# Choosing the next operation from one token, loading the odd strips earlier, and moving TensorE's fillers

## What is computed

```
x = x + _L0_conv_ref(_ln_c(x), ...)           # two convolutions, two L1-distance convolutions
t = _to_tokens(x)
t = t + _L0_ffn_ref(_ln_t(t), ...)            # the steps below
x = x + _L1_conv_ref(_ln_c(x), ...)           # two quantised convolutions
t = t + _L1_ffn_ref(_ln_t(t), ...)            # long filters over the tokens, mixed
```

```
op = jnp.argmax(h[0, 0, :NOPS])
...
y = jnp.einsum('bqk,bkd->bqd', attn, v) @ p['wo'][op]
h = jnp.where(p['am'][op], y, h)
z = jax.nn.relu(h @ p['w1'][op] + p['b1'][op]) @ p['w2'][op] + p['b2'][op]
h = jnp.where(p['fm'][op], z, h)
```

## Time and profile before

| | us |
|---|---|
| median of 3 runs | 351.51 |
| lowest and highest | 350.79, 351.81 |
| the profiled execution | 350.08 |
| its span, first to last instruction | 348.3 |
| TensorE busy in the span | 327.9 (94%) |
| the steps with their norm, 138 to 227 us | 89 |
| from the last choice to the second half of the norm's output | 12.4 |

### The profile page before, as it was taken

One profiled execution on the slowest core, in us unless ns is written; L12 is line 12 of the kernel. 1 busy time (PEld: TensorE's weight loads), 2 busy tenths in 40 slices (PEclk: granted clock), 3 DMA queues, 4 the chain that ended last, 5 costly groups with the idle time before them and its releaser, 6 DMA issues.

```text
span 348.3 us, 11982 instructions
## 1 busy us (share of the span) xinstructions
PE 327.9 (94%) x5193; PEld 209.5 (60%) x5193; DVE 249.7 (72%) x508; ACT 187.8 (54%) x213; POOL 21.6 (6%) x48
## 2 busy tenths in 40 slices
PE   8799899999999999979999999849899999999995
PEld 7436547754343334646564344327489999999994
DVE  1798999999999997543793976517556775564444
ACT  3871998787788892143775776431323233233221
POOL 4573000000000001100000000000000000000000
PEclk9999999999999999999999999969999999999999
DMA  5711900000000000910000000000014000000001
GB/s 178 225 25 19 366 32 2 2 3 0 2 2 2 2 2 0 360 29 17 3 2 0 2 4 2 0 9 0 0 38 107 8 3 6 4 4 5 4 6 49
DMA packets 12245, 13.24 MB, mean 38 GB/s; under 512 B 6026, under 2 KB 10908, under 8 KB 12184
## 3 DMA queue, kind: packets, MB, share of 16 engines
q1 hardware_dynamic: 11208, 9.17, 8.7%
q0 software_dynamic: 832, 3.00, 2.6%
q10 hardware_dynamic: 144, 0.20, 0.2%
HBM read 10.73 MB, written 0.40 MB: 32 GB/s over the span
## 4 chain that ended last, share of the span: by engine, by line
PE 54%; DVE 31%; SPq 7%; issue 4%; DMA 2%; ACT 2%; DVEq 1%; ACTq 0%
PE PS L1057 54%; DVE pool_ L854 18%; SPq L252 3%; DVE pool_ L936 1%; DMA W1R<-in_fwa 1%; DVE TMP L818 1%; DVE TMP L944 1%; DVE pool_ L965 1%; SPq L246 1%; SPq L255 1%; SPq L257 1%; DMA WA2R<-in_wa2r 1%; DVE pool_ L851 1%; SPq L259 1%; DVE MSC L767 0%
## 5 line engine op out<-in xcount | busy, mean ns | idle before, releaser
L1057 PE MATMUL PS<-pool_,CON 128*32 128x392 f32 (+2 forms) x1320 | 111.4, 493 | 0.7 <-ACT pool_ L522 0.2
L1057 PEld LDWEIGHTS PS<-pool_,CON 128*32 128x32 f32 (+1 forms) x1320 | 49.0, 110 | 60.8 <-issue 43.7
L472 ACT ACTIVATE pool_<-TMP,WA 128x3136 f32<-128x3136 f32 x26 | 75.4, 2927 | 11.0 <-PE PS L1057 10.8
L854 DVE TENSOR_SCALAR pool_<-TMP,WA 128x3136 f32<-128x3136 f32 x44 | 79.4, 1845 | 0.1
L571 ACT ACTIVATE pool_<-PS 128x272 f32<-128x272 f32 x64 | 25.5, 398 | 56.7 <-PE PS L1057 56.6
L1030 DVE TENSOR_TENSOR pool_<-PS,pool_ 128x128 f32<-128x128 f32 x64 | 18.6, 291 | 35.4 <-PE PS L1057 32.3
L1057 PE MATMUL PS<-HE,WS 128*32 128x136 f32 (+1 forms) x768 | 36.7, 317 | 0.2 <-ACT WS L563 0.2
L1057 PE MATMUL PS<-pool_,WS 128*32 128x136 f32 (+1 forms) x768 | 36.7, 316 | 0.0
L1057 PEld LDWEIGHTS PS<-pool_,WS 128*32 128x32 f32 x768 | 29.3, 109 | 2.7
L1057 PEld LDWEIGHTS PS<-HE,WS 128*32 128x32 f32 x768 | 28.9, 110 | 3.2 <-issue 0.4
L1057 PE MATMUL PS<-pool_,TMP 128*32 128x128 f32 x512 | 29.4, 272 | 0.0
(11 more groups left out here) (254 smaller groups left out, 375.9 us busy)
## 6 DMA issues: line engine op xcount, KB each, us to landing
pool_<-in_pho SPq DMA_DIRECT2D x1, 3144.0 KB, 11.9
HE<-in_phe SPq DMA_DIRECT2D x1, 3136.0 KB, 12.3
QZ<-CW SPq DMA_DIRECT2D x12, 98.0 KB
CW<-in_cw POOLq DMA_DIRECT2D x2, 576.0 KB, 4.7
CON<-in_con POOLq DMA_DIRECT2D x1, 732.5 KB, 5.5
out_y<-Y SPq DMA_DIRECT2D x1, 392.0 KB, 2.4
CQ<-in_ws SPq DMA_DIRECT2D x16, 9.0 KB
MPP<-in_mpp POOLq DMA_DIRECT2D x1, 256.0 KB, 3.1
```

Source lines behind the costliest of these rows:

```text
L472: a.activation(unit, window(n // CQ), ACT.Abs, bias=WA2[:, n:n + 1], scale=-1.0).then_inc(s["act_unit"], 1)
L854: v.tensor_scalar(unit, window(n // CQ), WA2[:, n:n + 1], None, ALU.max).then_inc(s["dve_unit"], 1)
L1057: return t.matmul(out_, lhsT, rhs, start=start, stop=stop, skip_group_check=True)
```

## The change

Five things are changed.

1. The choice is made earlier. The first is made from X1 (the norm doesn't move the largest entry) on bank 6 right after X1 is written, ahead of the norm; TensorE's small product for it stands between the two centring products. In attention a row is made from token 0 times the output weights. In the feed-forward part one column of H goes through `W1R`, ScalarE's relu (`TOK`, 128 x 1) and `W2S` on bank 7, and VectorE decides after its first unit. A step with both parts therefore decides twice, `decided` counts parts (`ops`) and not steps, and every engine waits for `decided` and counts `read_on` up before it loads KINT.
2. The squares, and CEN x H, are left for after the last step. CEN x X1 is made in the places of some fillers and at the end of each step.
3. In the feed-forward part banks 0 to 6 serve the units and unit 7 uses bank 0 again; ScalarE takes five units (0, 2, 3, 4, 6), VectorE three (1, 5, 7); the second layer goes to banks 2 and 3.
4. Fillers: 4 instead of 8, only ahead of step 1's feed-forward part and inside its branch; 8 instead of 2 in attention's.
5. `HO` now lies at the start of `pool_` under ring places 0 and 1, and is loaded when `ring_free` reaches NG - 3. SyncE loads W1R and W2S only when H of the feed-forward part before is written.

```
-WARM = dict(..., weights=8, ..., projections=2)
+WARM = dict(..., weights=4, projections=8)
...
+LEAD = NK * (NPH + 1) - 2 * NIMG * T
...
-            sp.wait_ge(s["ring_free"], NG)
+            sp.wait_ge(s["ring_free"], NG - 3)
             sp.dma_start(HO[:, :, :], ...)
...
                 with sp.If((c & 2) > 0):
+                    sp.wait_ge(s["ffn_h"], sp.snap(nf, min_val=0, max_val=NB) * 2 + 1)
...
         (ScalarE, a step)
-                    for u in range(0, 8, 2):
+                    a.wait_ge(s["tok_mm"], k + 1)
+                    a.activation(TOK[:, :], PS[:, 7, 0:1], ACT.Relu, bias=B1S).then_inc(s["tok_hid"], 1)
+                    for u in (0, 2, 3, 4, 6):
...
-                squares(n)
-                a.wait_ge(s["decided"], n + 1)
+                a.wait_ge(s["decided"], a.snap(ops, min_val=1, max_val=2 * NB) + 1)
+                a.sem_inc(s["read_on"], 1)
...
         (VectorE)
             v.wait_ge(s["x1_ready"], 2)
+            decide(1, 6)
             norm(1, X1, lambda h: half(H, h))
...
+                    decide(v.snap(ops, min_val=0, max_val=2 * NB) + 2, 6)
...
-                    for u in range(1, 8, 2):
+                    for u in (1, 5, 7):
                         v.wait_ge(s["ffn_h1"], k * 8 + (u + 1))
-                        v.tensor_scalar(HIDT[:, u, :], bank(u), ...)
+                        v.tensor_scalar(HIDT[:, u, :], bank(u % 7), ...)
+                        if u == 1:
+                            decide(v.snap(ops, min_val=0, max_val=2 * NB) + 2, 7)
...
         (TensorE, a step)
-                keep_warm(WARM["weights"])
...
+                    if not built:
+                        keep_warm(WARM["weights"])
                     t.wait_ge(s["ffn_wa"], k * 16 + 16)
-                    t.wait_ge(s["sx_sq"], n * 2)
+                    mm(PS[:, 7, 0:1], W1R[0:C, 0:HID], H[0:C, 0:1]).then_inc(s["tok_mm"], 1)
...
+                            if u == 6:
+                                t.wait_ge(s["decided"], t.snap(ops, min_val=0, max_val=2 * NB) + 1)
+                            if u == 7:
+                                t.wait_ge(s["hid_act"], k * 5 + 1)
...
+                            t.wait_ge(s["tok_hid"], k + 1)
+                            mm(PS[0:1, 7, ROW:ROW + C], TOK[:, 0:1], W2S[:, 0:C], True, False)
...
         (TensorE, after the last step)
+            for h in range(2):
+                mm(bank(4 + h), CEN[:, :], half(H, h), False, True).then_inc(s["sx_cent"], 1)
+            t.wait_ge(s["sx_sq"], 2)
```

151 lines of the change are left out of this document (76 added, 75 removed).

## The result

The changed kernel takes 354.97 us (median; 353.54 to 359.98) beside 351.15 us (350.53 to 351.81) of the kernel before, on the same chip. The ratio is 1.0097 with a 95% interval of 1.0059 to 1.0134: slower by about 1%, where 351.6 was forecast, with 353.1 as the range's upper end. A second series (after_again) gave 354.14 us and a ratio of 1.0117 (0.9997 to 1.0237).

A forecast was written before the change was run, and what follows sets the result against it. Bound by three waits of TensorE: before step 1's feed-forward part, before attention, and at the exit, with code fetch and half clock. Step 1 +0.1 and exit 0.0 gave 350.2 us profiled, 351.6 median; range 349.8 to 353.1.

The forecast's parts named there:

- the parts on the choice and its transfer: Step 1: KINT at 141.6 instead of 147.56, odd strips issued at 133.1, W1R landing at 147.1, 5.9 us earlier.
- The central claim: Step 1: TensorE's code comes only at 151.4, so units begin at 154.6, 0.95 us later despite early weights.
- The gap between fillers and unit 1 that was to show the packet's end: Step 1: a packet ends behind the fillers; unit 1 waits until 3.2 us after the first filler, 154.6.
- The last feed-forward part: Step 2's feed-forward part before the exit: forecast 0.7 us longer, within the last H's delay of 0.9 us.
- The new table load: ScalarE ahead of each feed-forward part: 1.28 us, fits into 2.41 us idle; with the skill's drain up to 0.6 us late.
- The exit, with the late H: 0.0 us: From the last H to XN's second half: no net change, XN at 238.3 as before, between -1.0 and +1.1.
- the outer end: Exit's slow bound, +1.1 us: the three fillers run at half clock again in front of the spread.
- the gain that pays for the rest: Exit: second packet comes while ScalarE squares, and fillers need not run at half clock; squares and late H eat it.
- Step 1 and its choices: +0.1 us: Step 1 up to attention's projections: start at 164.2 instead of 164.09, between +0.7 and -1.5.
- Rival C: Slower: work behind the jumps, at step 1 or exit, runs at half clock or without code; +1.1 to +2, 353.0; chance 0.22.
- Rival A: Faster: packet doesn't end as counted or the clock holds; step 1's units at 152.9; -1.5 us, 350.0; chance 0.22.
- B: Much faster: the weights' landing, not the jump, was step 1's wait; units at 149.8; -4 us, 347.5; chance 0.06.

The follow-up runs named there:

- no_fillers: Changed kernel without the four fillers (eight passes) behind step 1's jump: 353.9 us, ratio 1.0009 to the kernel before.
- fillers_at_exit: Changed kernel with eight more fillers behind TensorE's load of the choice, ahead of the jump out of the steps: 352.8 us, ratio 1.0024.
- early_jump: Changed kernel, TensorE's waits for H moved behind its KINT load to first use, eight fillers before both jumps, targets at packet starts: 345.2 us, ratio 0.9835.
- fillers_ahead: Changed kernel with eight fillers ahead of step 1's jump and two instead of eight ahead of the projections: 354.7 us, ratio 1.0084.
- early_bare_exit: early_jump without its eight fillers ahead of the jump out of the steps: 345.0 us, ratio 0.9800.
- early_shifted: early_jump with 112 unused passes that move both jump targets to places 229 and 231 of a packet: 351.5 us, ratio 0.9874.
- after: The changed kernel itself in its first series; its first profiled execution took 359.98 us, the median 354.97 us.
- warm_through: fillers_ahead with nine more fillers before TensorE's load of KINT and both jump targets at a packet's start: 352.6 us, ratio 1.0026.

## Why the prediction was wrong

Right were the parts on the choice and its transfer. KINT was forecast for 141.6 and stood at 141.8; `W1R`'s issue for 143.6 (143.90), the odd strips' for 133.1 (132.61), their landing 10.6 us later. The central claim held too: TensorE cannot use the early weights, because its code is late. The jump's code was forecast for 151.4 and came at 152.07, the fillers ran at half clock as said and ended at 154.95 (154.2; eight passes of 0.39 from 151.4, as the prediction has them, would end at 154.5, which its sum doesn't use), and the units began 1.3 us later than before (0.95). The gap between fillers and unit 1 that was to show the packet's end is not there: the first pass follows the fillers at once, since they lasted until about 3 us behind the first of them (152.07). It takes no_fillers to show it. The last feed-forward part took 0.69 us more, as forecast (0.7). The new table load in front of it fits, and `TOK` is not late; ScalarE's rows:

```profile
220.14 1.28 ACT L534 ACT_TABLE_LOAD   x1
221.44 0.20 ACT L534 ACTIVATE WSM<-CON 128x1 f32<-128x1 f32 x1
221.98 0.26 ACT L538 ACTIVATE TOK<-PS,W2S 128x1 f32<-128x1 f32 x1 [0.34 <-PE PS L1062]
```

The first use of the engine comes 20 ns behind the load, so the drain of 1.38 us that the Trainium skill (ScalarE: Activation LUTs, What ACT_TABLE_LOAD costs) adds is not to be seen here either.

Where it failed, first: **"The exit, with the late H: 0.0 us"**. The sum there was H at 226.45, code 4.35 us behind it, 1.6 us for the first half's product, then 5.9: 11.85 us from H to XN. Measured were 14.52. Of the 2.7 us missing, 0.4 are the code (4.73 behind H), and the rest is the clock, as fillers_at_exit shows, which by full clock alone takes 11.78: I took one half for the centring product alone and full clock from the variance on, but it was at one half until 241. The three fillers took 2.33 us in front of the spread, which I had put down as the outer end, and the spread's passes were 0.43 us a pair instead of 0.22, which stood in no case at all. Behind this lies a misreading of the earlier trace rows. I saw that the pause behind 13 passes would be hidden and called that the gain that pays for the rest. Without that pause the kernel before needs 10.41 us, not 12.80. The exit's new order, products and squares behind the code, cost 2.0 to 3.5 us together with the clock behind it, and the packet's place gave only 2.4 back. How much of that is the order and how much the clock, these single executions don't separate.

Second: **"Step 1 and its choices: +0.1 us"**, measured +1.25. Three small terms add up, none of which is a new mechanism: the code 0.67 later, which put the units 0.35 later than forecast; the part 5.98 us from its first pass to H instead of 5.6, since its first passes were still at half clock (ten in 1.53 us, 1.14 at step 2); and 1.47 us from H to the first filler of attention where I took 1.0 from the range 0.9 to 1.6.

Rival C was what happened, but its price, 353.0, took one place or the other. Both happened, with the spread at half clock on top. Its point of decision, the granted clock reading one half when unit 1 or the variance begins, was met at both, and it should have had more than 0.22: the earlier trace rows showed the exit at half clock after 2.5 us of standstill, and the change made the standstills 6.0 and 3.9 us long. Rival A fell with the clock; B fell with the first pass at 152 us and with early_jump, where the packet moves with the jump. The Trainium skill (Runtime: NRT & Kernel Launch, Instruction fetch mechanics) gives TensorE's instruction memory 2048 instructions, which B leans on; but the same section says that it is refilled in order by blocks of 256 instructions, and that a branch taken out of a window of two blocks waits for a fetch. The traces agree with the latter: a packet moved at both far jumps, at 149.3 and 229.4 in the changed kernel.

Left open: what exactly takes the clock, and so how much of each loss one execution shows. 2.08 us of standstill were followed by one half in fillers_ahead, and 2.38 us were not in early_bare_exit. By the same code one execution held it and another did not: early_jump's step 1 ran at 1.00 throughout, and early_bare_exit's, which is the same, had units at half (15.75 to the projections instead of 13.28).

## What to carry to other kernels

An early decision is worth little to an engine that must still wait for data before it may load the decision: put the load and the jump ahead of the data's wait, and let the data be awaited at its first use. Whatever is moved behind a far jump waits for the code, here about 3 us, and then runs on a clock that the waiting may have halved; leave ahead of the jump what another engine can work on meanwhile. Before reading a pause as the cost of an order of instructions, look whether it is only where a packet of code ends; 28 instructions of padding on a path that isn't taken were worth 1% here.

## What was not expected of the hardware

- TensorE's code comes in packets of 256 instructions, 16 KB each (45 packets hold 0.74 MB, and 28 instructions of padding moved a pause away). A jump to code that isn't there shows its first instruction 2.4 to 3.4 us after the packet moved, and the packet behind it is usable 2.6 to 3.5 us after that first instruction (2.58 to 3.51 in nine pauses of seven kernels). The second packet is late because it moves only when the jump's target runs: 0 to 0.9 us behind the first pass in every trace looked at (152.3 against 152.07 in the changed kernel). The count of passes before the pauses follows from counting instructions in the built program; in early_shifted both counts, ten and four plus eight, were forecast and met.
- Attention has a stretch of some 10 us at half clock in five of the traces (after, no_fillers, warm_through, early_shifted, early_bare_exit), though TensorE is busy throughout; it makes attention 60.0 to 60.4 us long instead of 56.2 to 57.4. No trace of the kernel before has it, but its times fall into two groups as well, mostly 350 to 352.5 and 354 to 356 us, the second at a lower mean clock (0.97 against 0.99). In the first profile of the changed kernel (columns as above), where it begins in 188 to 189:

```profile
189.00:190.00 1.00, 1.00 (x10) 0.48 (x6) 0.00 (x0) 0.00 (x0) 0.00 (x0) 0.50 0.00 0
...
199.00:200.00 1.00, 1.00 (x12) 0.33 (x12) 0.81 (x1) 0.06 (x1) 0.00 (x0) 1.00 0.00 0
```
- The same code of step 1 took 19.18 to 20.83 us in five kernels, with the moment at which full clock returned. Differences under 1% between kernels that stand still for several us are therefore hard to measure: the changed kernel's interval is 1.0059 to 1.0134 in one series and 0.9997 to 1.0237 in the other.
